# Pair attention on one core: two-chunk bursts, two-step products, and a rebuilt beginning and tail

## The chip, the core and the metric

The kernel runs on 1 core of one Trainium2 chip. The metric is device time in microseconds (us); lower is better. Everything is computed in 32-bit floats.

## The reference: what is computed

The input `r_x` is (2048, 40, 64): 2048 batches of 40 fields with 64 numbers each. For each batch all 780 pairs of fields are formed, and

```
inner  = x[:, ROW, :] * x[:, COL, :]                   # 780 products of 64 numbers
h      = relu(inner @ W1.T + b1)                       # 64 hidden units a pair
logits = h @ W2.T + b2                                 # one number a pair
attn   = softmax(logits, axis=1)                       # over the 780 pairs
pooled = sum(inner * attn, axis=1)
y      = pooled @ Wl.T + bl                            # one number a batch
```

## The kernel before, in words

Two batches lie beside each other in the 128 partitions (64 + 64 embedding numbers); such a pair is a *duo*, and there are 1024. A *step* is two duos (`STEP_DUOS`), so there are 512 steps. A *chunk* is 8 steps or 16 duos, a *round* is 32 steps or 4 chunks; there are 64 chunks and 16 rounds. The pairs are ordered by the distance between the fields: shifts 1 to 19 are full windows of 20, shift 20 is a rest of 10, and each duo's 780 pairs are two halves of 390 (`HALF`).

Per step:
- VectorE (`products`) writes the products into a ring `inner` of 8 steps: two instructions of 2 x 380 elements, and in every odd step one more of 80 for shift 20 of two steps.
- TensorE (`first_layer`, called for half 0 and half 1) multiplies them by `w1_block` in 64x32 tiles of the array. Each call is 16 matmul records of 390 columns and fills one *slot*.
- ScalarE (`relu`) empties the slot into `hidden`, 780 elements a half.
- TensorE (`score`) multiplies `hidden` of the step before by W2, again 16 records, and adds into `logit_bank`; a round's 32 steps fill its rows.

Per chunk, between two steps:
- `turn_chunk`: five 128x128 transposes bring a loaded chunk of `x_rows` into a slot; ScalarE (`copy_turned`) copies it to the ring `xt` (3 chunks), and VectorE (`extend`, `scale_rows`) repeats the first 20 fields behind the 40 and writes `x_scaled` = x times Wl.
- `gram_matrix`: 64 matmul records of 40 columns in 64x64 tiles give each batch's scaled inner products of all fields, into a slot; ScalarE (`copy_gram`) copies them to `gram_rows`, and 12 DMAs (`store_gram`) write them to memory in the order in which the softmax needs them. `load_gram` reads a round's back.

Per round: `softmax_of_round` and `sums_of_round` on VectorE, `exp_of_round` on ScalarE; maxima and sums go to `stats`. After the last round eight transposes turn `stats`, and a chain of small VectorE operations on 16 partitions merges the halves and writes `y_out`.

The order of all work is written out by hand. PSUM has three slots of two banks (`SLOTS = 3`), taken in turn by everything that TensorE writes except the scores; `place` lists the order, the counters `slots_filled` and `slots_emptied` follow it, and `wait_for_slot` makes TensorE wait until the slot of three places before has been emptied. Turns and grams stand in the loop over steps:

```
TURN_AT = -13
GRAM_AT = -5
SPREAD_AT = -3
gram_after = {max(n * CHUNK_STEPS + GRAM_AT, 1 + n): n for n in range(CHUNKS)}
turn_after = {n * CHUNK_STEPS + TURN_AT: n for n in range(2, CHUNKS)}
```

so that from step 11 on a turn and a gram follow each other after every step s with s % 8 = 3; this is called a *burst* here. At the beginning SyncE issues both halves of chunk 0, eight small loads and chunk 1 in one queue; TensorE turns chunk 0, transposes W1, turns chunk 1, and only then starts step 0. The waits of VectorE on TensorE's reading of `inner` let it run at most 8 steps ahead.

Of the kernel before, what the change touches and what calls it, by code (L numbers as in the profile page):

```python
# [6 lines left out]
ALU = mybir.AluOpType  # L7
# [3 lines left out]
P = 128  # L11
# [8 lines left out]
def pair_attention_kernel(nc, x, w1, b1, w2, b2, wl, bl, y):  # L20
# [30 lines left out]
    INNER_RING = 8  # L51
    XT_RING = 3
    SLOTS = 3

# [9 lines left out]
    with ExitStack() as ctx:  # L64
# [20 lines left out]
        x_scaled = sb("x_scaled", [P, CHUNK_DUOS * FIELDS])  # L85
# [13 lines left out]
        maxima = sb("maxima", [ROUNDS, STEP_DUOS, 2, P // 2])  # L99
        top = sb("top", [ROUNDS, STEP_DUOS, P // 2])  # L100
        down = sb("down", [ROUNDS, STEP_DUOS, 2, P // 2])
        scale = sb("scale", [ROUNDS, STEP_DUOS * P])
        part = sb("part", [ROUNDS, 3, STEP_DUOS * P])
        total = sb("total", [ROUNDS, 3, P])
        weighted_sum = sb("weighted_sum", [ROUNDS, P])
        inverse = sb("inverse", [ROUNDS, P])
        ratio = sb("ratio", [ROUNDS, P])
        y_out = sb("y_out", [ROUNDS, P])
# [8 lines left out]
        ident_ready = sem("ident_ready")  # L117
        w1_loaded = sem("w1_loaded")
# [29 lines left out]
        def inner_to(s):  # L148

            return 5 * (s // 2 + 1)  # L150


        TURN_AT = -13
        GRAM_AT = -5
        SPREAD_AT = -3

        gram_after = {max(n * CHUNK_STEPS + GRAM_AT, 1 + n): n for n in range(CHUNKS)}
        turn_after = {n * CHUNK_STEPS + TURN_AT: n for n in range(2, CHUNKS)}
        spread_after = {max(n * CHUNK_STEPS + SPREAD_AT, 1 + n): n for n in range(1, CHUNKS)}


        place = {("turn", 0): 0, ("weights", 0): 1, ("turn", 1): 2}
        for s in range(STEPS):
            place["layer", s, 0] = len(place)
            place["layer", s, 1] = len(place)
            if s in turn_after:
                place["turn", turn_after[s]] = len(place)
            if s in gram_after:
                place["gram", gram_after[s]] = len(place)
# [10 lines left out]
        EXP_AT = [4, 5]  # L180
        SUMS_AT = [13, 14]
# [3 lines left out]
        y_dram = y.rearrange("(a r k) o -> r a (k o)", a=2, k=ROUND_DUOS)  # L185
# [4 lines left out]
        def _(sp):  # L190
# [29 lines left out]
            load_chunk(0)  # L220
# [14 lines left out]
            for n in range(CHUNKS):  # L235
                if n + 2 < CHUNKS:
                    sp.wait_ge(slots_filled, count_to("turn", n))
                    load_chunk(n + 2)
                store_gram(n)
                if n % CHUNKS_PER_ROUND == CHUNKS_PER_ROUND - 1:  # L240
                    load_gram(n // CHUNKS_PER_ROUND)
# [13 lines left out]
        def _(pe):  # L255
# [12 lines left out]
            def gram_matrix(n):  # L268
                pe.wait_ge(scaled_ready, n + 1)
                wait_for_slot("gram", n)  # L270
                for m in range(GRAM_PAIRS):
                    for j in range(2):
                        duo = 2 * m + j
                        for ab in range(2):
# [4 lines left out]
                                x_scaled[rows, duo * FIELDS:(duo + 1) * FIELDS],  # L279
# [61 lines left out]
            for n in range(4 * STEP_DUOS):  # L341
                last = nc.tensor.transpose(slot[0][0:ROUNDS, n * P:(n + 1) * P], stats[:, n, :], ident[:, :])  # L342
            last.then_inc(stats_turned, 1)

        @block.scalar
        def _(act):
# [27 lines left out]
            def exp_of_round(r, j):  # L374
                if j == 0:
                    act.wait_ge(bias_ready, r + 1)
# [180 lines left out]
```

## Time and profile before

| what | value |
|---|---|
| median of 3 runs | 1144.26 us (1144.24 to 1145.02) |
| the profiled execution's own time | 1142.66 us |
| its span | 1140.8 us |
| TensorE busy | 1117.5 us, 98% |
| VectorE busy | 1053.8 us, 92% |
| ScalarE busy | 981.2 us, 86% |

The span is from the first to the last event of the program on the core; the run's own time is 1.86 us longer. PE is TensorE's matmul, PEld its weight load, DVE is VectorE, ACT is ScalarE, POOL is GpSimd, SPq is the queue of SyncE, which issues DMAs. L296 is line 296 of the kernel: L264 is the transpose of `turn_chunk`, L277 the matmul of `gram_matrix`, L296 that of `first_layer`, L316 that of `score`, L325 the transpose of W1, L342 that of `stats`; L431 and L438 are the products, L369 is the relu, L353 and L361 are the copies of a turned chunk and of a gram.

### The profile page before, as it was taken

Reading aid. Unit: us, or ns where it says so; the run is one execution under the profiler, and the core shown is the slowest. Engines: PE = TensorE matmul, PEld = TensorE weight load, DVE = VectorE, ACT = ScalarE, POOL = GpSimd, SP = SyncE. Lnnn points to the kernel's source line nnn. Section 1 sums busy time; section 2 is a strip of 40 time slices with the busy share of each in tenths; the row PEclk is TensorE's granted clock in tenths of the full one; section 3 lists DMA queues with packets and bytes.
Section 4 is the critical chain, followed back from the end, with each engine's and each line's share of the span. In section 5 each row is a group of like instructions: output and inputs, shape, how many; then the busy total and the mean of one; then the engine's idle time right before and its main releaser. Section 6 shows DMA issues by size and latency. Waiting matters only on the chain.

```text
span 1140.8 us, 63299 instructions
## 1 busy us (share of the span) xinstructions
PE 1117.5 (98%) x29001; PEld 550.5 (48%) x29001; DVE 1053.8 (92%) x1691; ACT 981.2 (86%) x1219; POOL 0.7 (0%) x6
## 2 busy tenths in 40 slices
PE   6999999999999999999999999999999999999995
PEld 3445444444444444454544544554444444544442
DVE  7999999998999989999899998999999899998983
ACT  5888888888988888888888888888889888898884
POOL 0000000000000000000000000000000000000000
PEclk9999999999999999999999999999999999999998
DMA  2231211312212221122212113122131221222110
GB/s 58 39 70 26 67 30 35 67 29 63 41 29 63 41 56 35 29 65 39 58 35 68 29 34 70 28 64 41 25 67 36 58 39 29 63 41 57 23 25 23
DMA packets 220376, 51.31 MB, mean 45 GB/s; under 512 B 216016, under 2 KB 216016, under 8 KB 220112
## 3 DMA queue, kind: packets, MB, share of 16 engines
q1 hardware_dynamic: 220112, 47.27, 20.2%
q8 instruction: 229, 3.75, 1.4%
q14 instruction: 35, 0.29, 0.1%
HBM read 34.11 MB, written 13.12 MB: 41 GB/s over the span
## 4 chain that ended last, share of the span: by engine, by line
PE 98%; DVE 1%; SPq 1%; DMA 0%; ACT 0%; issue 0%; ACTq 0%
PE slot L296 60%; PE logit_bank L316 30%; PE slot L277 4%; PE slot L264 4%; DMA x_rows<-in_r_x 0%; PE slot L342 0%; SPq L193 0%; ACT hidden L369 0%; DVE weighted L468 0%; SPq L223 0%; SPq L227 0%; SPq L225 0%; SPq L230 0%; DVE logits L448 0%; DVE row_max L452 0%
## 5 line engine op out<-in xcount | busy, mean ns | idle before, releaser
L369 ACT ACTIVATE hidden<-slot,b_col 128x780 f32<-128x780 f32 x1024 | 874.7, 909 | 118.5 <-PE slot L296 118.5
L431 DVE TENSOR_TENSOR inner<-xt 128x760 f32<-128x760 f32 x1024 | 907.8, 943 | 51.3 <-PE slot L296 50.8
L296 PE MATMUL slot<-inner,w_block 64*32 64x390 f32 x16384 | 781.4, 489 | 0.0
L296 PEld LDWEIGHTS slot<-inner,w_block 64*32 64x32 f32 x16384 | 314.1, 107 | 331.0 <-issue 271.3
L316 PE MATMUL logit_bank<-hidden,w_window 64*32 64x390 f32 x8192 | 442.9, 487 | 0.6 <-ACT hidden L369 0.6
L316 PEld LDWEIGHTS logit_bank<-hidden,w_window 64*32 64x32 f32 x8192 | 155.3, 105 | 183.5 <-ACT hidden L369 85.6
L353 ACT COPY xt<-slot 128x640 f32<-128x640 f32 x64 | 44.3, 692 | 20.4 <-PE slot L264 20.4
L264 PE MATMUL slot<-ident,x_rows 128*128 128x128 f32 x320 | 50.1, 288 | 9.7 <-DMA x_rows<-in_r_x 9.7
L438 DVE TENSOR_TENSOR inner<-xt 128x80 f32<-128x80 f32 x256 | 59.4, 232 | 0.0
L264 PEld LDWEIGHTS slot<-ident,x_rows 128*128 128x128 f32 x320 | 34.6, 143 | 49.5 <-issue 44.1
L277 PE MATMUL slot<-xt,x_scaled 64*40 64x40 f32 x4096 | 52.9, 205 | 0.0
L277 PEld LDWEIGHTS slot<-xt,x_scaled 64*40 64x40 f32 x4096 | 45.4, 117 | 11.7 <-issue 11.7
L361 ACT COPY gram_rows<-slot 128x640 f32<-128x640 f32 x64 | 44.4, 693 | 5.9 <-PE slot L277 0.4
L418 DVE TENSOR_SCALAR x_scaled<-xt,wl_col 128x640 f32<-128x640 f32 x64 | 34.8, 544 | 0.0
L448 DVE COPY logits<-logit_bank 128x780 f32<-128x780 f32 x16 | 15.5, 970 | 20.5 <-PE logit_bank L316 20.5
L468 DVE CUSTOM_DVE_ANT_1 weighted<-weight,gram 128x380 f32<-128x380 f32 x32 | 28.0, 874 | 0.8 <-ACT weight L377 0.8
L409 DVE COPY xt<-xt 128x320 f32<-128x320 f32 x64 | 20.3, 317 | 5.8 <-ACT xt L353 5.8
L377 ACT ACTIVATE weight<-logits,exp_bias 128x390 f32<-128x390 f32 x32 | 19.9, 622 | 3.6 <-DVE exp_bias L460 3.6
L452 DVE TENSOR_REDUCE row_max<-logits 128x2 f32<-128x780 f32 x16 | 15.5, 966 | 0.5
L476 DVE CUSTOM_DVE_ANT_0 weighted<-weight,gram 64x10 f32<-64x10 f32 x64 | 10.8, 169 | 1.0
L342 PE MATMUL slot<-ident,stats 128*16 128x128 f32 x8 | 1.9, 416 | 6.0 <-DVE stats L483 6.0
L377 ACT ACTIVATION_READ_ACCUMULATOR weight<-logits,exp_bias 128x1 f32 x32 | 6.4, 201 | 0.0
(28 smaller groups left out, 27.0 us busy)
## 6 DMA issues: line engine op xcount, KB each, us to landing
x_rows<-in_r_x SPq DMA_DIRECT2D x128, 160.0 KB, 3.1
gram<-gram_dram SPq DMA_DIRECT2D x32, 400.0 KB, 3.8
gram_dram<-gram_rows SPq DMA_DIRECT2D x512, 12.5 KB
gram_dram<-gram_rows SPq DMA_DIRECT2D x256, 25.0 KB
w_rows<-in_L_rec_W SPq DMA_DIRECT2D x2, 16.0 KB, 2.3
wl_col<-in_L_rec_Wl SPq DMA_DIRECT2D x2, 0.2 KB, 2.3
b_col<-in_L_rec_b SPq DMA_DIRECT2D x2, 0.2 KB, 2.3
w_window<-in_L_rec_W SPq DMA_DIRECT2D x2, 0.2 KB, 2.3
```

The lines of the kernel that those rows point to most:

```text
L264: last = nc.tensor.transpose(banks_of("turn", n)[:, t * P:(t + 1) * P], x_rows[n % 2][:, t, :, :].rearrange("p h e -> p (h e)"), ident[:, :])
L277: last = nc.tensor.matmul(banks_of("gram", n)[j * TILE:j * TILE + FIELDS, at:at + FIELDS], x_scaled[rows, duo * FIELDS:(duo + 1) * FIELDS] ...
L296: last = nc.tensor.matmul(banks[to:to + QUAD, ab * BANK:ab * BANK + HALF], w1_block[rows, of:of + QUAD], inner[rows, at:at + HALF], start= ...
L316: last = nc.tensor.matmul(logit_bank[g * QUAD:(g + 1) * QUAD, j * BANK:j * BANK + HALF], w2_window[rows, first:first + QUAD], hidden[s % R ...
L353: nc.scalar.copy(window_view(xt[n % XT_RING], 0, [[EXT, CHUNK_DUOS], [TT, U], [1, TT]]), window_view(banks_of("turn", n), 0, [[U, CHUNK_DU ...
L361: nc.scalar.copy(gram_rows[n % 2][:, :, :, :].rearrange("p a m n -> p a (m n)"), banks_of("gram", n)[:, :].rearrange("p (a n) -> p a n", a ...
L369: nc.scalar.activation(hidden[s % RING][:, half * PAIRS:(half + 1) * PAIRS].rearrange("p (a n) -> p a n", a=2), banks_of("layer", s, half) ...
L377: nc.scalar.activation(weight[:, j * HALF:(j + 1) * HALF], logits[:, j * HALF:(j + 1) * HALF], ACT.Exp, bias=exp_bias[:, j:j + 1], accum_o ...
L418: nc.vector.tensor_scalar(x_scaled[:, :].rearrange("p (d f) -> p d f", f=FIELDS), whole[:, :, 0:FIELDS], wl_col[:, 0:1], None, ALU.mult).t ...
L431: nc.vector.tensor_tensor(window_view(inner, to + half * HALF, [[PAIRS, STEP_DUOS], [SPAN, SHIFTS], [1, SPAN]]), window_view(fields, at + ...
L438: nc.vector.tensor_tensor(window_view(inner, to + SHIFTS * SPAN, [[PAIRS, duos], [HALF, 2], [1, LAST]]), window_view(fields, at, [[EXT, du ...
L468: nc.vector.tensor_tensor_reduce(out=weighted[:, 0:main].rearrange("p (d i) -> p d i", i=SPAN), in0=weight[:, of:of + main].rearrange("p ( ...
```

## The change

Five parts; the core of the diff stands below.
1. **Bursts of two chunks.** Chunks are taken in groups of 2. After steps 4, 20, 36, ... stand two turns and then two grams, where before one turn and one gram stood after every eighth step. `xt` gets 4 chunks instead of 3, `x_scaled` gets 2 buffers. SyncE stores the grams of both chunks one after the other (24 DMAs), then loads the next two chunks.
2. **Products of two steps.** In even steps VectorE makes the products of two steps, with two instructions of 4 x 380 elements and one of 80 between them. The ring `inner` has 16 steps. TensorE waits on `inner_ready` in both halves of each step.
3. **Beginning.** The second half of chunk 0 is loaded by ScalarE's queue. 14 transposes of the identity into `logit_bank` stand before the turn of chunk 0, and 14 more before step 0. Chunk 1 is turned after step 1. Chunk 0 is copied in two parts (4 duos, then 12), `extend_first` treats the first, and the products of steps 0 and 1 are made singly, with shift 20 of both behind the first instruction.
4. **Softmax of rounds.** The exponentials stand 3 and 7 steps into the next round instead of 4 and 5, the sums 15 and 21 instead of 13 and 14. In the last round there is no copy of the logits: each of the two columns of duos has its own maximum and bias, read from `logit_bank`, and ScalarE reads `logit_bank` too.
5. **Tail.** One matmul (64x64 tile, 128 columns) moves the upper 64 partitions of `stats` to the lower ones, and the merging runs on 64 partitions with 32 to 96 elements in each. `y` is stored by two DMAs whose pieces are 2 numbers (8 bytes), 512 pieces each, where one DMA had 32 pieces of 256 bytes.

```diff
-    INNER_RING = 8
-    XT_RING = 3
+    INNER_RING = 16
+    XT_RING = 4
+    GROUP = 2
     SLOTS = 3
+    FIRST_DUOS = 4
+    WARM_UP = [14, 14]
...
+        GROUP_STEPS = GROUP * CHUNK_STEPS
+        TURN_AT = -12
+        GRAM_AT = TURN_AT + GROUP_STEPS
+        SPREAD_AT = [-1, 3]
...
+        gram_after = {g * GROUP_STEPS + GRAM_AT: g for g in range(CHUNKS // GROUP)}
+        turn_after = {g * GROUP_STEPS + TURN_AT: chunks_of(g) for g in range(1, CHUNKS // GROUP)}
+        turn_after[1] = range(1, GROUP)
+        spread_after = {n // GROUP * GROUP_STEPS + SPREAD_AT[n % GROUP]: n for n in range(1, CHUNKS)}
...
-        EXP_AT = [4, 5]
-        SUMS_AT = [13, 14]
+        EXP_AT = [3, 7]
+        SUMS_AT = [15, 21]
...
-            load_chunk(0)
+            sp.dma_start(x_rows[0][:, :, 0, :], x_chunks[0, 0]).then_inc(x_loaded[0], 16)
...
+            for group in range(CHUNKS // GROUP):
+                for n in chunks_of(group):
+                    if n + 2 < CHUNKS:
+                        sp.wait_ge(slots_filled, count_to("turn", n))
+                        load_chunk(n + 2)
+                for n in chunks_of(group):
+                    store_gram(n)
+                    if n % CHUNKS_PER_ROUND == CHUNKS_PER_ROUND - 1:
+                        load_gram(n // CHUNKS_PER_ROUND)
...
             def first_layer(s, half):
-                if half == 0:
-                    pe.wait_ge(inner_ready, inner_to(s))
+                pe.wait_ge(inner_ready, inner_to(s, half))
...
+            def warm_up(count):
+                for _ in range(count):
+                    nc.tensor.transpose(logit_bank[:, 0:P], ident[:, :], ident[:, :])
             pe.wait_ge(ident_ready, 2)
+            warm_up(WARM_UP[0])
             turn_chunk(0)
             pe.wait_ge(w1_loaded, 2 * 16)
             nc.tensor.transpose(banks_of("weights", 0)[:, 0:P], w1_rows[:, :], ident[:, :]).then_inc(slots_filled, 1)
-            turn_chunk(1)
+            warm_up(WARM_UP[1])
...
                 if s in turn_after:
-                    turn_chunk(turn_after[s])
+                    for n in turn_after[s]:
+                        turn_chunk(n)
                 if s in gram_after:
-                    gram_matrix(gram_after[s])
+                    for n in chunks_of(gram_after[s]):
+                        gram_matrix(n)
...
-            for n in range(4 * STEP_DUOS):
-                last = nc.tensor.transpose(slot[0][0:ROUNDS, n * P:(n + 1) * P], stats[:, n, :], ident[:, :])
-            last.then_inc(stats_turned, 1)
+            upper = slice(TILE, P)
+            nc.tensor.matmul(slot[0][0:TILE, 0:4 * STEP_DUOS * ROUNDS], ident[upper, upper],
+                             stats[upper, :, :].rearrange("p n r -> p (n r)"), start=True, stop=True,
+                             tile_position=(TILE, 0)).then_inc(stats_turned, 1)
...
+            act.dma_start(x_rows[0][:, :, 1, :], x_chunks[1, 0]).then_inc(x_loaded[0], 16)
...
+            def shifts_to_19(to, at, duos, fields, half):
+                nc.vector.tensor_tensor(
+                    window_view(inner, to + half * HALF, [[PAIRS, duos], [SPAN, SHIFTS], [1, SPAN]]),
+                    window_view(fields, at + half * SPAN, [[EXT, duos], [0, SHIFTS], [1, SPAN]]),
+                    window_view(fields, at + half * SPAN + 1, [[EXT, duos], [1, SHIFTS], [1, SPAN]]),
+                    ALU.mult).then_inc(inner_ready, 1)
+            def first_products():
+                dve.wait_ge(xt_ready, 1)
+                for s in range(2):
+                    for half in range(2):
+                        shifts_to_19(s * STEP, s * STEP_DUOS * EXT, STEP_DUOS, xt[0], half)
+                        if s == 0 and half == 0:
+                            shift_20(0, 0, 2 * STEP_DUOS, xt[0])
             def products(s):
                 n, in_chunk = s // CHUNK_STEPS, s % CHUNK_STEPS
-                if in_chunk == 0:
-                    dve.wait_ge(xt_ready, n + 1)
+                if in_chunk == 0 or s == 2:
+                    dve.wait_ge(xt_ready, n + 2)
                 if s >= INNER_RING:
-                    dve.wait_ge(slots_filled, count_to("layer", s - INNER_RING, 1))
+                    dve.wait_ge(slots_filled, count_to("layer", s + 1 - INNER_RING, 1))
+                fields, duos = xt[n % XT_RING], 2 * STEP_DUOS
...
                 for half in range(2):
+                    shifts_to_19(to, at, duos, fields, half)
+                    if half == 0:
+                        shift_20(to, at, duos, fields)
...
+            def softmax_of_last_round(r):
+                dve.wait_ge(steps_scored, STEPS)
+                dve.wait_ge(exp_done, 2 * r)
+                for j in range(STEP_DUOS):
+                    nc.vector.reduce_max(row_max[:, j:j + 1], logit_bank[:, j * BANK:j * BANK + HALF], AX_X).then_inc(
+                        max_ready, 1)
...
-            chain(nc.vector.tensor_copy(maxima[:, :, :, :], maximum))
-            chain(nc.vector.tensor_tensor(top[:, :, :], maxima[:, :, 0, :], maxima[:, :, 1, :], ALU.max))
+            chain(nc.vector.tensor_tensor(top[:, :, :], maximum[0], maximum[1], ALU.max))
+            for half in range(2):
+                nc.vector.tensor_tensor(down[:, half, :, :], maximum[half], top[:, :, :], ALU.subtract).then_inc(
+                    down_ready, 1)
...
-            sp.dma_start(y_dram, y_out[:, :].rearrange("r (a k) -> r a k", a=2)).then_inc(y_stored, 16)
-            sp.wait_ge(y_stored, 16)
+            for a in range(2):
+                sp.dma_start(y_dram[a], y_out[a * QUAD:(a + 1) * QUAD, :, :]).then_inc(y_stored, 16)
+            sp.wait_ge(y_stored, 2 * 16)
```

## Rows read from the trace of the kernel before

**Rows 1.** The page, part 4: shares of the span on the chain that ended last.
```profile
PE 98%; DVE 1%; SPq 1%; DMA 0%; ACT 0%; issue 0%; ACTq 0%
```

**Rows 2.** Waits over the whole span: us in total, times, longest us.
```profile
DVE inner L431 <- PE slot L296: 50.8, 75, 1.6
```

**Rows 3.** Groups by form: busy us, mean ns of one, then idle before them.
```profile
L277 PE MATMUL slot<-xt,x_scaled 64*40 64x40 f32 x4096 | 52.9, 205 | 0.0
L264 PE MATMUL slot<-ident,x_rows 128*128 128x128 f32 x320 | 50.1, 288 | 9.7 <-DMA x_rows<-in_r_x 9.7
```

**Rows 4.** Timeline around one burst: start us, us, then engine, line and operation.
```profile
523.23 0.86 PE L316 MATMUL logit_bank<-hidden,w_window 64*32 64x390 f32 x16
...
523.88 1.52 PE L296 MATMUL slot<-inner,w_block 64*32 64x390 f32 x32
...
524.91 1.71 ACT L369 ACTIVATE hidden<-slot,b_col 128x780 f32<-128x780 f32 x2 [0.25 <-PE slot L296]
525.20 0.87 PE L316 MATMUL logit_bank<-hidden,w_window 64*32 64x390 f32 x16
...
525.99 0.77 PE L264 MATMUL slot<-ident,x_rows 128*128 128x128 f32 x5
...
526.69 0.83 PE L277 MATMUL slot<-xt,x_scaled 64*40 64x40 f32 x64
526.79 0.69 ACT L353 COPY xt<-slot 128x640 f32<-128x640 f32 x1 [0.17 <-PE slot L264]
...
527.45 1.54 PE L296 MATMUL slot<-inner,w_block 64*32 64x390 f32 x32
```

**Rows 5.** Timeline of the first 26 us.
```profile
0.74 1.35 SPq L193 DMA_DIRECT2D x_rows<-in_r_x  x2
...
1.17 0.29 POOL L251 TENSOR_SCALAR_AFFINE_SELECT ident<-ident 128x128 f32<-128x128 f32 x1 [0.23 <-POOL ident L249]
...
4.76 1.30 PE L264 MATMUL slot<-ident,x_rows 128*128 128x128 f32 x5 [4.76 <-DMA x_rows<-in_r_x]
...
5.86 0.42 PE L325 MATMUL slot<-ident,w_rows 128*128 128x128 f32 x1
...
6.10 0.69 ACT L353 COPY xt<-slot 128x640 f32<-128x640 f32 x1 [4.08 <-PE slot L264]
...
7.18 3.53 DVE L431 TENSOR_TENSOR inner<-xt 128x760 f32<-128x760 f32 x4
...
12.51 3.68 PE L296 MATMUL slot<-inner,w_block 64*32 64x390 f32 x64
...
25.12 1.52 PE L296 MATMUL slot<-inner,w_block 64*32 64x390 f32 x32
```

**Rows 6.** Timeline of the queue of SyncE near the end: the last gram's stores, the last load.
```profile
1101.50 5.70 SPq L204 DMA_DIRECT2D gram_dram<-gram_rows  x12
1110.40 0.82 SPq L216 DMA_DIRECT2D gram<-gram_dram  x2
```

**Rows 7.** Timeline of the tail, from the last score on.
```profile
1126.10 0.97 DVE L448 COPY logits<-logit_bank 128x780 f32<-128x780 f32 x1 [15.94 <-PE logit_bank L316]
...
1128.63 0.62 ACT L377 ACTIVATE weight<-logits,exp_bias 128x390 f32<-128x390 f32 x1 [3.58 <-DVE exp_bias L460]
...
1129.38 0.84 DVE L468 CUSTOM_DVE_ANT_1 weighted<-weight,gram 128x380 f32<-128x380 f32 x1 [0.78 <-ACT weight L377]
...
1131.97 1.88 PE L342 MATMUL slot<-ident,stats 128*16 128x128 f32 x8 [5.97 <-DVE stats L483]
1133.88 0.41 DVE L520 COPY maxima<-slot 16x256 f32<-16x256 f32 x1 [1.97 <-PE slot L342]
1134.33 0.28 DVE L521 TENSOR_TENSOR top<-maxima 16x128 f32<-16x128 f32 x1
...
1137.41 0.94 DVE L533 RECIPROCAL inverse<-total 16x128 f32<-16x128 f32 x1
...
1139.01 0.34 SPq L244 DMA_DIRECT2D out_y<-y_out  x1
```

More of the change, by code:

```diff
@@ L84, in pair_attention_kernel @@
         inner = sb("inner", [P, INNER_RING * STEP])
-        x_scaled = sb("x_scaled", [P, CHUNK_DUOS * FIELDS])
+        x_scaled = [sb(f"x_scaled{s}", [P, CHUNK_DUOS * FIELDS]) for s in range(GROUP)]
         gram_rows = [sb(f"gram_rows{s}", [P, 2, GRAM_PAIRS, FIELDS]) for s in range(2)]
@@ L146, in pair_attention_kernel, with inner_to, chunks_of @@
                                    kind="Internal").ap()
[L148 to L162, printed above, removed]
+        def inner_to(s, half):
+            return 2 + half + (2 * s if s < 2 else 3 * (s // 2) + 2)
+        GROUP_STEPS = GROUP * CHUNK_STEPS
+        TURN_AT = -12
+        GRAM_AT = TURN_AT + GROUP_STEPS
+        SPREAD_AT = [-1, 3]
+        def chunks_of(group):
+            return range(group * GROUP, (group + 1) * GROUP)
+        gram_after = {g * GROUP_STEPS + GRAM_AT: g for g in range(CHUNKS // GROUP)}
+        turn_after = {g * GROUP_STEPS + TURN_AT: chunks_of(g) for g in range(1, CHUNKS // GROUP)}
+        turn_after[1] = range(1, GROUP)
+        spread_after = {n // GROUP * GROUP_STEPS + SPREAD_AT[n % GROUP]: n for n in range(1, CHUNKS)}
+        place = {("turn", 0): 0, ("weights", 0): 1}
         for s in range(STEPS):
@@ L166, in pair_attention_kernel @@
             if s in turn_after:
-                place["turn", turn_after[s]] = len(place)
+                for n in turn_after[s]:
+                    place["turn", n] = len(place)
             if s in gram_after:
-                place["gram", gram_after[s]] = len(place)
+                for n in chunks_of(gram_after[s]):
+                    place["gram", n] = len(place)
         def count_to(*what):
@@ L509, in _ @@
             dve.wait_ge(stats_turned, 1)
-            rounds = slice(0, ROUNDS)
-            maximum = slot[0][rounds, 0:2 * P].rearrange("r (j h s) -> r j h s", j=STEP_DUOS, h=2)
-            sums = slot[0][rounds, 2 * P:8 * P].rearrange("r (n q) -> r n q", n=3)
-            chained = [ROUNDS]
+            lower = slice(0, TILE)
+            pairs = STEP_DUOS * ROUNDS
+            moved = slot[0][lower, 0:4 * pairs]
+            maximum = [stats[lower, 0:STEP_DUOS, :], moved[:, 0:pairs].rearrange("p (j r) -> p j r", j=STEP_DUOS)]
+            sums = [stats[lower, STEP_DUOS:4 * STEP_DUOS, :].rearrange("p (n j) r -> p n (j r)", n=3),
+                    moved[:, pairs:4 * pairs].rearrange("p (n q) -> p n q", n=3)]
+            chained = [ROUNDS - 1 + STEP_DUOS]
             def chain(instruction):
@@ L518, in chain @@
                 dve.wait_ge(dve_chain, chained[0])
[L520 to L531 removed]
+            chain(nc.vector.tensor_tensor(top[:, :, :], maximum[0], maximum[1], ALU.max))
+            for half in range(2):
+                nc.vector.tensor_tensor(down[:, half, :, :], maximum[half], top[:, :, :], ALU.subtract).then_inc(
+                    down_ready, 1)
+            dve.wait_ge(scale_ready, 1)
+            for half in range(2):
+                last = nc.vector.tensor_tensor(part[:, half, :, :], sums[half],
+                                               window_view(scale, half * pairs, [[0, 3], [1, pairs]], lower), ALU.mult)
+                if half == 0:
+                    last.then_inc(dve_chain, 1)
+                    chained[0] += 1
+            chain(last)
+            chain(nc.vector.tensor_tensor(total[:, :, :], part[:, 0, :, :], part[:, 1, :, :], ALU.add))
             chain(nc.vector.tensor_tensor(weighted_sum[:, :], total[:, 1, :], total[:, 2, :], ALU.add))
```

129 lines of the change are left out of this document (66 added, 63 removed).

## The prediction, made before the change was run

> **What bounds the kernel now.** I read the page first, its chain that ended last: 98% of it is TensorE's matmul [rows 1]. Then the waits: VectorE, the next busiest engine, waits 50.8 us for TensorE to give back parts of the ring `inner` [rows 2], so it runs ahead and TensorE sets the pace. ScalarE too waits before each pair of relus [rows 4]. What counts is therefore the time from one TensorE instruction group to the next, and I took that from the timeline around one burst [rows 4]: a score takes 0.65 us (523.23 to 523.88), the two halves of a layer 1.32 us (to 525.20), a step 1.97 us. A burst takes 2.25 us from the score before it to the next layer (525.20 to 527.45), less the score's own 0.65: 1.60 us. That splits into 0.14 before the turn (525.99 less 525.20 less 0.65), 0.70 from turn to gram and 0.76 from gram to layer. Then the two ends: TensorE starts step 0 at 12.51 us [rows 5], and from 1126.10 us, when the last score has ended, there is a serial chain of 14.7 us to the end of the span at 1140.8 [rows 7]. The sum below is made against the span of 1140.8 and the execution's own 1142.66 us; the median is 1144.26, 1.60 above the latter, and I subtract the same saving from it.
>
> **Part 1, bursts of two chunks.** What do two turns in a row cost? The five transposes last 0.77 us together and one lasts 0.288 on average [rows 3, 4], so they start every (0.77 - 0.288)/4 = 0.12 us. Two turns are 0.70 + 5 x 0.12 = 1.30 us, against 2 x 0.70 apart. The gram's 64 records start every (0.83 - 0.205)/63 = 0.0099 us [rows 3, 4]: two grams are 0.76 + 64 x 0.0099 = 1.39 us against 1.52. The 0.14 ahead of the turn is paid once instead of twice. A double burst is 0.14 + 1.30 + 1.39 = 2.83 us against 3.20: 0.37 saved. From the start of step 5 on, before has 61 full bursts (turns of chunks 3 to 63) and one of a gram alone (0.14 + 0.76 = 0.90): 98.5 us. After has 30 double ones and one with two grams alone (1.53): 86.4 us. Saving **12.1 us**, of which one turn has only moved to the beginning, where I count it. The lower bound: the 0.10 and 0.13 within a pair aren't a change of tile shape but something that each turn and gram pays (its wait, its new slot). Then only the 0.14 goes, after has 30 x 3.06 + 1.66 = 93.5, and the saving is 5.0. I take the upper value, since 0.12 and 0.0099 are what the trace shows inside a turn and a gram, and I see nothing else that changes at a seam except the tile shape.
>
> Does the burst now stall? Four places in a row need four slots and there are three. From the layer's start [rows 4]: relus end at about +1.9 and +2.74 (524.91 + 1.71 less 523.88), turn a starts +2.11, turn b +2.71 (needs the first relu), gram a +3.41 (needs the second), gram b +4.04. Gram b needs the copy of turn a: a copy starts 0.80 after its turn (526.79 less 525.99) and lasts 0.69, so it ends at +3.60. That is 0.44 us spare, the thinnest place. The next layer at +4.80 needs the copy of turn b, which ends at +4.3. Nothing stalls, and ScalarE is caught up when the next relu is due. The exponential now comes one step ahead of a burst (3 into a round, burst after 4); it puts ScalarE back by 0.75 us (1128.63 to 1129.38 [rows 7]) less the 0.25 idle that each step has [rows 4]: 0.5, gone again by the copies, since turn a's copy then ends at about +3.9. Priced at nothing; if it isn't hidden it costs up to 0.3 in 15 rounds, 4 us at most.
>
> SyncE: 12 stores take 5.70 us, the wait for their landing lasts until 1110.40, 3.2 us after the last issue, and the load is 0.82 [rows 6]. With 24 stores (11.7 us) the queue holds up the loads of the next two chunks, but these have a burst period of 16 x 1.97 + 2.83 = 34.3 us; loads behind stores end after some 22. The last round: stores begin about 2 us later and last 6 us longer, so the gram load is issued at about 1118.5 in the time of before and lands some 4 us later. Its reader comes at about 1128: hidden with 5 us to spare.
>
> **Part 2, products of two steps.** Four instructions of 760 elements take 3.53 us. An elementwise operation costs 1.05 ns an element (0.41 less 0.28 us for 128 elements more, a copy and a maximum of two tensors) and 0.15 fixed [rows 7], part of it overlapped, so one of 1520 saves at most 0.1 of two of 760. That frees VectorE by up to 512 x 0.1 = 50 us and gives TensorE nothing: it isn't on the chain. Priced at nothing. The cover is VectorE's lead of several steps; without it each step pair would wait for 3.5 us of products against 3.93 us of TensorE, so even then it keeps up. The second wait of `first_layer` finds its count reached and is nothing too. The softmax sits at the same step, where VectorE waits for the score of the round anyway, with a lead of 7 to 8 steps.
>
> **Part 3, beginning.** Chunk 0's halves were issued one behind the other, 1.35 us for both, and TensorE started at 4.76 [rows 5]. Two queues bring the second 0.7 earlier at best, to 4.1. But the warm-up starts when the identity is there (1.46 us) and its 14 transposes start every (1.30 - 0.42)/4 = 0.22 us: 3.1 us, so the turn starts at 4.6. Its slot was ready 1.34 later in before (6.10) and 0.80 later in the middle of the kernel; I take 1.1, so 5.7. The part copy (about 0.30) and the part extension (about 0.25) put the first product at 6.3 instead of 7.18. Products go at 0.86 each, shift 20 at 0.2: step 0 ready at 7.4 and 8.25 (its two halves), step 1 at 9.1 and 9.95; extension 0.3; then steps 2 and 3 together, half 0 by 12.1, half 1 by 13.75; scaling, extension and scaling 1.3; steps 4 and 5, half 0 by 16.9, half 1 by 18.6. TensorE is bound by VectorE here. It starts (2,1) at 13.8, ends score 1 at 15.1, step 3 with score 2 at 17.05, has to wait until 18.6 for (4,1), ends score 3 at 19.9 and the double burst at 22.75. Before, step 5 starts at 25.12 [rows 5]. Saving **2.3 us**, range 1.5 (x no earlier, all cold) to 3.0. From step 5 on TensorE has work: VectorE needs 3.5 us for two steps and TensorE 3.93.
>
> The clock: the transposes of chunk 0 and the first layers run at half rate in before. The 64 records from 12.51 last 3.68 us [rows 5], where two layers of a step in the middle last 1.32 each; the granted clock is recorded as full, the durations are those of 1.2 GHz. If the warm-up has no effect, its second half ends at 5.9 + 0.3 + 14 x 0.22 = 9.3, steps 0 and 1 lose another 0.85, and step 2 starts at about 14.2 instead of 12.1; but VectorE gives (4,1) at 18.6 in any case, and the double burst ends at 22.9 to 23.7. So the clock is worth 0.2 to 1.0 us here. The Trainium skill (TensorE: Matmul & The Clock Gate, Part 4) says that transposes do not count as busy for the clock gate. This case's before neither proves nor refutes it: the layers from 12.51 us were still slow, and what opened the clock during them can't be read off. By the rule the sum would be 17.4 less 0.2 to 1.0.
>
> **Part 5 and the last round.** VectorE after the last score: before 3.28 us to the first sum (1126.10 to 1129.38) [rows 7]: copy 0.97, maximum 0.97, two small ones 0.52, exponential 0.75. After: twice a maximum of 390 (0.56 by the rate above), two small ones and gaps, 1.12 each: 2.25. The first exponential starts at 1.12 and is there at 1.9. Saves 1.0. Moving `stats`: 1.91 before (1131.97 to 1133.88); one matmul of 128 columns is two records, 0.42 + 0.22 cold [rows 5]: 0.7, saves 1.2. Merging: before 5.13 us (1133.88 to 1139.01). After: six operations of 32 elements at 0.18, three of 96 at 0.25, the reciprocal (0.94 at 128) at about 0.35, the exponential 0.3, gaps 0.3: 2.9, saves 2.2; if fixed costs are higher (0.28 each) 1.2. Storing y: before 1.8 us from issue to the span's end. Two issues add 0.4; the landing of 512 pieces of 8 bytes isn't in the trace. Below: nothing more. Above: like the last gram store, 3.2 us instead of 1.45, plus 1.75. I take +1.1 in all, between 0.4 and 2.2, nearer to the many small pieces of the gram. The Trainium skill (DMA: Bandwidth & Descriptors, Specifications) says that writes below 512 B become read-modify-writes; both forms of the store lie below that, so it doesn't tell them apart. Tail: 1.0 + 1.2 + 2.2 - 1.1 = **3.3 us**, range 1.5 to 4.6.
>
> **The sum.** 12.1 + 2.3 + 3.3 = 17.7, less 0.3 for what the exponentials ahead of bursts may cost: 17.4. Span 1123.4, own time 1125.3, median 1144.26 - 17.4 = **1126.9 us**.
>
> **Rivals.**
> - *Seams cost what they did* (only the 0.14 goes): 7.1 less, 1134.0. For it: each turn has its own wait on a DMA and on a slot. Against: nothing of these was late in the trace. Chance 0.13.
> - *The warm-up doesn't open the clock*, the rule above: the first layers last 1.3 us a half, 1127.1 to 1127.9. Chance 0.2.
> - *The two-chunk burst stalls on the three slots.* Place: gram b waits for ScalarE's copy of turn a. With 0.44 us spare it costs nothing; if the copies come x later than that, 31 bursts cost 31x, and from x = 0.56 the gain is gone, from 0.63 it is slower by over 0.2%. A full copy behind each relu pair too late (2 x 0.69) gives 1126.9 + 43 = 1170. Chance 0.03.
> - *Part of it is given back at the ends*: no earlier x, y landing over 2 us, merging dear: 1130.5. Chance 0.1.
> - *No net change*: seams as before and both ends gain nothing, under 3 us of gain. Chance 0.03; nothing in the profile speaks for it.
> - The forecast: 0.51.
>
> Range 1123.5 to 1133: it leaves out the first, third and fifth, 0.19. A difference under 0.2% (2.3 us) is what a measurement can't tell from none. Faster 0.94, within 0.03, slower 0.03.
>
> **What would show it.** In a middle double burst: ten transposes and then 128 gram records; from the score to the next layer 0.65 + 2.83 us. 3.06 instead of 2.83 is the first rival; idle time before L277 with ScalarE's copy as releaser is the third. Start of step 5's layer at 22.75. Layer groups of 0.65 us a half in steps 0 and 1 mean an open clock. From the last score to the first issue of y's store 8.5 us (12.9 before), then 2.9 to the end. VectorE's busy time falls by some 30 to 50 us and its waits grow by as much. I would be wrong if VectorE's lead is lost after the beginning, so that TensorE waits on `inner` in the middle.

## The result: 1.3% slower, and the profile after

| | before | after |
|---|---|---|
| median | 1144.25 us (4 runs, 1143.76 to 1145.02) | 1159.26 us (4 runs, 1157.5 to 1159.69) |
| span of the profiled execution | 1140.8 us | 1157.9 us |

The ratio is 1.0129, 95% interval 1.0114 to 1.0144. I had predicted 1126.9 us (1123.5 to 1133) and gave slower a chance of 0.03.

The page of the changed kernel, parts 1, 3 and 4, beside [rows 1]:
```profile
PE 1124.2 (97%) x29023; PEld 638.7 (55%) x29023; DVE 1008.3 (87%) x1185; ACT 980.0 (85%) x1220; POOL 0.7 (0%) x6
...
q8 instruction: 231, 3.78, 1.4%
...
PE 93%; DVE 4%; issue 2%; ACT 0%; POOLq 0%; POOL 0%; ACTq 0%
```
TensorE still carries the chain, but 2% of the span is now "issue": time in which it waited for nothing that the profile shows. (The line gives VectorE 4%, but in the middle of the kernel no idle time of TensorE's matmuls has VectorE as releaser.) VectorE's busy time fell by 45 us, as foreseen, and buys nothing.

The waits of the changed kernel (us in total, times, longest us):
```profile
DVE logits L503 <- PE logit_bank L331: 108.9, 15, 9.4
...
PE slot L311 <- issue: 10.0, 12, 1.7
...
PE slot L293 <- issue: 6.0, 4, 2.1
...
PE slot L311 <- DVE inner L470: 1.2, 2, 0.7
```
VectorE waits for TensorE longer than before [rows 2]; TensorE waits for VectorE 1.2 us in all, in the beginning. Between the beginning and the last steps no idle time of its matmuls names an engine.

**Where the 17.1 us of span come from.** I split the span at two places: the start of step 5, and the end of the last score as VectorE sees it. A *period* is the 16 steps from the start of one burst's turns to the next; periods are numbered by their burst, and the one that starts at 20.03 us is number 2. Timelines of the changed kernel, the beginning and one double burst in the middle:
```profile
1.51 3.25 PE L340 MATMUL logit_bank<-ident 128*128 128x128 f32 x14 [1.51 <-POOL ident L267]
4.56 1.27 PE L280 MATMUL slot<-ident,x_rows 128*128 128x128 f32 x5
5.62 0.42 PE L346 MATMUL slot<-ident,w_rows 128*128 128x128 f32 x1
5.84 2.07 PE L340 MATMUL logit_bank<-ident 128*128 128x128 f32 x14
...
12.34 0.89 PE L311 MATMUL slot<-inner,w_block 64*32 64x390 f32 x16
13.94 0.89 PE L311 MATMUL slot<-inner,w_block 64*32 64x390 f32 x16 [0.72 <-DVE inner L470]
...
18.56 0.89 PE L311 MATMUL slot<-inner,w_block 64*32 64x390 f32 x16 [0.45 <-DVE inner L470]
19.23 0.87 PE L331 MATMUL logit_bank<-hidden,w_window 64*32 64x390 f32 x16
20.03 1.31 PE L280 MATMUL slot<-ident,x_rows 128*128 128x128 f32 x10
...
22.68 1.54 PE L311 MATMUL slot<-inner,w_block 64*32 64x390 f32 x32
```
```profile
53.52 0.86 PE L331 MATMUL logit_bank<-hidden,w_window 64*32 64x390 f32 x16
...
54.31 1.31 PE L280 MATMUL slot<-ident,x_rows 128*128 128x128 f32 x10
...
55.55 1.61 PE L293 MATMUL slot<-xt,x_scaled 64*40 64x40 f32 x128
...
57.10 1.54 PE L311 MATMUL slot<-inner,w_block 64*32 64x390 f32 x32
```
- Beginning: step 5 starts at 22.68 us instead of 25.12 [rows 5]: 2.4 us gained.
- The double burst at 20 us takes 22.68 less 19.23 less the score's 0.65 = 2.80 us against 2 x 1.60 [rows 4]; the one at 54 us is a little disturbed and takes 57.10 less 53.52 less 0.65 = 2.93. The 16 steps from burst to burst take 34.28 us where nothing goes wrong (34.43 with a softmax), against 2 x 17.35 = 34.70 before (17.50 for the half with a softmax). Gained, as in the plan: some 0.4 us a period.
- But only 9 of the 30 periods take up to 34.5 us. The 30 periods from 20.03 us on take 1060.6 us together; at 34.28, with 0.15 for each of 15 softmaxes, they would take 1030.7. That is 30 us lost, and the stretch behind them (38.09 us to the next burst) loses 3.7 more: **34 us in all**. The 19 idle times described below add up to 25 of them, and two stretches at half clock (3.4 us each) cost some 3.4; the remaining 5 to 6 us are small delays that I can't assign one by one. From step 5 to the last score the kernel takes 1121.5 us instead of 1101.0, 20.5 more, where I had predicted 12.1 less.
- Tail: 13.8 us from 1144.14 to the end, against 14.7.

This is what a lost microsecond looks like, in the timeline of the changed kernel, TensorE alone:
```profile
265.81 0.60 PE L280 MATMUL slot<-ident,x_rows 128*128 128x128 f32 x4
266.34 1.48 PE L293 MATMUL slot<-xt,x_scaled 64*40 64x40 f32 x128
269.48 1.55 PE L311 MATMUL slot<-inner,w_block 64*32 64x390 f32 x32 [1.66 <-issue]
```
and here twice as long, with the windows view of that place (us, then busy us of PE, PEld, DVE, ACT, POOL, the granted clock, DMA share, GB/s):
```profile
442.50 1.34 PE L293 MATMUL slot<-xt,x_scaled 64*40 64x40 f32 x115
445.94 0.35 PE L293 MATMUL slot<-xt,x_scaled 64*40 64x40 f32 x13 [2.10 <-issue]
446.22 2.25 PE L311 MATMUL slot<-inner,w_block 64*32 64x390 f32 x32
```
```profile
443.60:447.00 3.40, 1.30 (x63) 0.82 (x59) 3.40 (x4) 1.18 (x2) 0.00 (x0) 0.99 0.19 27
447.00:450.00 3.00, 3.00 (x48) 1.21 (x40) 3.00 (x5) 1.85 (x3) 0.00 (x0) 0.50 0.33 49
```
The second idle time falls in the middle of a gram, between records of one loop that has no wait in it. No slot, no copy, no VectorE can be late there. Behind it the granted clock was 0.50 (1.2 GHz) for some 3 us, which makes this the most expensive period (38.33 us).

**The theory.** The page has a queue q8 of kind "instruction": 231 packets of 16384 bytes. TensorE has 59218 records (matmuls, weight loads, semaphore instructions), 256.4 for each packet; before, 58662 and 229, 256.2. So q8 brings TensorE's instructions in blocks of 256. A double burst is 20 + 256 of them, the grams' 256 within 1.4 us. I looked up, for each time over 0.5 us between the starts of two records in a row, which record of the stream (modulo 256) came after it, and how long before that the last q8 packet had ended. Worked out from the trace of the changed kernel:
```
at us   idle us  record mod 256   us since the end of a q8 packet
 92.86   1.34        193            1.41
267.75   1.73        193            1.25
408.43   1.47        193            1.41
443.64   2.30        193            1.47
729.99   1.70        193            1.39
765.10   1.80        193            1.26
```
From step 5 to the last steps there are 19 such idle times outside the stretches of half clock, all at record 193, resumed 1.25 to 1.59 us after a packet. Before the change there is none over 0.5 us from step 5 to the last steps. The shortest time in which 256 records in a row start is 3.08 us before and 1.27 after.

The order of the packets says how far ahead TensorE's instructions are. Counted from 0, packet n of the changed kernel begins at the earliest 0.2 us before record 256n + 193 starts, in the middle 0.7 us after it, at most 4.4. In each of the 19 cases the packet that ended last is the one that had begun after the record 193 before, and its own length was 0.9 to 1.3 us. So the trace shows one block held ahead: from one record 193 to the next TensorE needs the packet's late start, its length and another 1.25 to 1.59 us, and the quickest such stretch took 2.87 us. All 18 stretches in which TensorE used up its 256 records in under 2.9 us ended in an idle time (0.43 to 2.3 us).

The theory, **instruction supply**: a block that is used up in less than about 3 us leaves TensorE waiting for the next. Rivals: the 24 gram DMAs behind a burst delay these packets (*store contention*); four places in a row on three slots (*slots*); the long VectorE instructions, the ring of 16 or the second wait of a step (*products*).

### The profile page after: what moved, and what is told of

It reads as the page before. It is cut to its first block, busy times and chain, and to the rows that moved or that the text cites. A ratio compares the mean times of both kernels' runs of the same rounds, so it can differ in the third digit from the quotient of the medians.

```text
span 1157.9 us, 63334 instructions
## 1 busy us (share of the span) xinstructions
PE 1124.2 (97%) x29023; PEld 638.7 (55%) x29023; DVE 1008.3 (87%) x1185; ACT 980.0 (85%) x1220; POOL 0.7 (0%) x6
## 4 chain that ended last, share of the span: by engine, by line
PE 93%; DVE 4%; issue 2%; ACT 0%; POOLq 0%; POOL 0%; ACTq 0%
PE slot L311 57%; PE logit_bank L331 28%; PE slot L293 4%; PE slot L280 3%; DVE inner L470 3%; DVE weighted L536 0%; PE logit_bank L340 0%; DVE inner L463 0%; DVE x_scaled L459 0%; ACT hidden L396 0%; DVE row_max L522 0%; DVE weighted L544 0%; DVE xt L450 0%; PE slot L366 0%; DVE round_stats L525 0%
## 5 line engine op out<-in xcount | busy, mean ns | idle before, releaser
L311 PE MATMUL slot<-inner,w_block 64*32 64x390 f32 x16384 | 870.3, 489 | 11.1 <-issue 10.0
L470 DVE TENSOR_TENSOR inner<-xt 128x1520 f32<-128x1520 f32 (+1 forms) x514 | 874.6, 1728 | 0.6
L311 PEld LDWEIGHTS slot<-inner,w_block 64*32 64x32 f32 x16384 | 387.4, 107 | 326.8 <-issue 220.3
L331 PE MATMUL logit_bank<-hidden,w_window 64*32 64x390 f32 x8192 | 531.1, 488 | 1.9 <-issue 1.3
L331 PEld LDWEIGHTS logit_bank<-hidden,w_window 64*32 64x32 f32 x8192 | 191.3, 105 | 143.9 <-issue 52.8
L293 PE MATMUL slot<-xt,x_scaled 64*40 64x40 f32 x4096 | 48.9, 205 | 6.0 <-issue 6.0
L379 ACT COPY xt<-slot 128x640 f32<-128x640 f32 (+1 forms) x65 | 41.4, 689 | 6.7 <-PE slot L280 6.7
L280 PE MATMUL slot<-ident,x_rows 128*128 128x128 f32 x320 | 42.7, 280 | 0.0
L450 DVE COPY xt<-xt 128x320 f32<-128x320 f32 (+1 forms) x64 | 20.3, 317 | 0.0
L409 ACT ACTIVATE weight<-logits,exp_bias 128x390 f32<-128x390 f32 x30 | 18.6, 620 | 0.0
L340 PE MATMUL logit_bank<-ident 128*128 128x128 f32 x28 | 5.3, 367 | 1.5 <-POOL ident L267 1.5
```

The source lines that it names most:

```text
L280: last = nc.tensor.transpose(banks_of("turn", n)[:, t * P:(t + 1) * P], x_rows[n % 2][:, t, :, :].rearrange("p h e -> p (h e)"), ident[:, :])
L293: last = nc.tensor.matmul(banks_of("gram", n)[j * TILE:j * TILE + FIELDS, at:at + FIELDS], x_scaled[n % GROUP][rows, duo * FIELDS:(duo + 1 ...
L311: last = nc.tensor.matmul(banks[to:to + QUAD, ab * BANK:ab * BANK + HALF], w1_block[rows, of:of + QUAD], inner[rows, at:at + HALF], start= ...
L331: last = nc.tensor.matmul(logit_bank[g * QUAD:(g + 1) * QUAD, j * BANK:j * BANK + HALF], w2_window[rows, first:first + QUAD], hidden[s % R ...
L379: copied = nc.scalar.copy(window_view(xt[n % XT_RING], first * EXT, [[EXT, last - first], [TT, U], [1, TT]]), window_view(banks_of("turn", ...
L450: nc.vector.tensor_copy(whole[:, duos, FIELDS:EXT], whole[:, duos, 0:SPAN]).then_inc(xt_ready, 1)
```

## The experiments

All times are medians beside runs of the kernel before on the same chip (1143.8 or 1144.2); ratios are to that kernel.

**e1: the second gram four steps later.**
```diff
-        gram_after = {g * GROUP_STEPS + GRAM_AT: g for g in range(CHUNKS // GROUP)}
+        for g in range(CHUNKS // GROUP):
+            gram_after[g * GROUP_STEPS + GRAM_AT] = [g * GROUP]
+            gram_after[g * GROUP_STEPS + GRAM_AT + 4] = [g * GROUP + 1]
```


> The changed kernel, but the second gram of each pair stands 4 steps later (after steps 8, 24, 40, ... instead of 4, 20, 36, ...), so that no burst has more than 20 + 128 TensorE instructions. Instruction supply (TensorE runs out of instructions in and just behind a burst of 276 in 2.8 us): the 32 us of stalls vanish, and what is left is the beginning (2.4 us), the tail (0.9) and the seams that still go (31 pairs by about 0.1): 1144.3 - 6.5 = about 1138 us. Store contention (the DMAs of the grams delay TensorE's instructions): the same DMAs still follow, in two parts; some stalls stay, 1143 to 1155. Long vector instructions or the ring of 16 steps: nothing changes there, 1158 to 1160.

Measured: 1136.3 us, ratio 0.9933 (0.9918 to 0.9948). 26 of 30 periods are 34.55 or 34.70 us within 0.1. Moving 128 of 276 instructions is enough; three idle times over 0.5 us are left, each at record 193. There the 256 records had taken 4.2 to 4.8 us, but the packet had begun 2.5 to 2.7 us late.

**e2: the stores later.**
```diff
             def store_gram(n):
+                if n < CHUNKS - GROUP:
+                    sp.wait_ge(slots_emptied, count_to("layer", n // GROUP * GROUP_STEPS + GRAM_AT + 3, 1))
```


> The changed kernel, but SyncE starts the 24 stores of a pair of grams only when the relus of the third step behind the burst are done, some 8 us later; the last pair is stored as before. Instruction supply: the stalls lie 4 to 6 us behind the start of a burst whatever the stores do, 1158 to 1160 us. Store contention: the stalls vanish or move behind the stores; if they vanish 1159.3 - 32 = 1127, if they move no less than half stay, and they then lie 10 us or more behind the start of a burst.

Measured: 1155.3 us (1153.0 to 1159.6), ratio 1.0113 (1.0092 to 1.0134). The timelines of TensorE and of SyncE's queue around one burst (it began at 89.8 us):
```profile
92.77 0.52 PE L313 MATMUL slot<-inner,w_block 64*32 64x390 f32 x6
94.14 1.17 PE L313 MATMUL slot<-inner,w_block 64*32 64x390 f32 x18 [0.84 <-issue]
```
```profile
100.75 3.56 SPq L219 DMA_DIRECT2D gram_dram<-gram_rows  x9
```
TensorE starts again 4.4 us into the burst, 6.6 us before the first store. Store contention isn't the cause. The runs scatter by 6.6 us and the median lies 4 below the changed kernel's; the profiled execution has 18 idle times at 193, no period over 36.4 us and no half clock. Whether the stores add something to single stalls stays open.

**e3: bursts of one chunk, the rest as changed.**
```diff
+        gram_after = {max(n * CHUNK_STEPS - 5, 3 + 2 * n): [n] for n in range(CHUNKS)}
+        turn_after = {n * CHUNK_STEPS - 13: [n] for n in range(2, CHUNKS)}
+        turn_after[1] = [1]
```
SyncE stores each chunk's gram by itself again, as in the kernel before.

> The changed kernel with one-chunk bursts where the kernel before has them (a turn and a gram after every eighth step); all the rest as changed: double products, ring of 16, beginning, tail. Instruction supply: no stalls in the middle; beginning 2.4 and tail 0.9 us better than before: about 1141 us. Long vector instructions or the doubled waits of the first layer as cause: the stalls stay, 1150 to 1162.

Measured: 1139.1 us, ratio 0.9959 (0.9944 to 0.9974); no idle time over 0.5 us. Everything but the double bursts together is a gain of 4.7 us.

**e4: products of single steps.**
```diff
                 for half in range(2):
-                    shifts_to_19(to, at, duos, fields, half)
-                    if half == 0:
-                        shift_20(to, at, duos, fields)
+                    shifts_to_19(to, at, STEP_DUOS, fields, half)
+                if s % 2:
+                    shift_20(to - STEP, at - STEP_DUOS * EXT, 2 * STEP_DUOS, fields)
```


> The changed kernel, but from step 2 on VectorE makes the products of single steps and TensorE waits on them once a step, as before; bursts, ring size, beginning and tail as changed. Instruction supply and store contention: 1158 to 1161 us, stalls as in the changed kernel. Long vector instructions or the second wait of a step as cause: about 1127 to 1130 us. VectorE's waits for TensorE shrink by some 35 us in any case.

Measured: 1157.5 us, ratio 1.0124 (1.0105 to 1.0143), 18 idle times, all at 193. The kernel differs from its description in one thing: the wait instruction in the second half stayed, with a count that is already reached. e11 is free of it.

**e5: half of each gram, same places.**
```diff
-                for m in range(GRAM_PAIRS):
+                for m in range(0, GRAM_PAIRS, 2):
```


> The changed kernel with its double bursts, but every second pair of duos is left out of the grams (64 TensorE records of a pair of grams instead of 128, so 148 instructions in a burst instead of 276); half of the gram values are therefore old contents of the slots. The burst still takes four places of three slots and the same copies and stores. Instruction supply: the work left out is 32 x 0.63 = 20 us and the 32 us of stalls vanish too, 1159.3 - 52 = about 1107 us, every period of 16 steps 33.65 us. Slots (TensorE waits for ScalarE because four places in a row need three slots): the stalls stay, about 1139 us.

Measured: 1112.3 us (two runs). No idle time over 0.5 us; 28 of 30 periods are 33.87 or 34.0 us. The work left out is 0.41 us a period, not 0.63, 13 us in all; 1159.3 less 13 less the 34 lost gives 1112. With the stalls kept it would be 1146. The burst still has four places in a row on three slots, so slots are out.

**e6: the same kernel, 128 instructions later.**
```diff
-    WARM_UP = [14, 14]
+    WARM_UP = [14, 78]
```


> The changed kernel with 64 more transposes of the identity ahead of step 0, so that everything behind them stands 128 instructions later in TensorE's stream; nothing else. Instruction supply in blocks of 256 instructions (16384 bytes): in the changed kernel the periods of 16 steps whose burst begins at instruction 50 to 200 of a block are 34.9 to 38.3 us and those at 203 to 31 are 34.3 to 34.8. Shifted by 128, the periods that were long become short and the other way round (those that began at 203 to 31 now begin at 75 to 159 and are 35.3 or more); the time is 1159 + 7 for the transposes = about 1166. A cause that lies in the work (slots, DMA, VectorE, the round) leaves the long periods where they are.

Measured: 1163.5 us (two runs), 17 idle times over 0.5 us, all at record 193 again. Nothing of the work behind step 0 differs, yet the long periods are others. Worked out from both traces, the period's number with the record (modulo 256) at which its burst begins and its length in us:
```
period      changed kernel      e6
   2         31   34.28      159   36.12
   6          0   34.28      128   35.96
  10        226   34.28       98   35.03
   8        113   35.51      241   34.29
  17        110   37.24      238   34.43
  26        106   35.62      234   34.30
```
This is the test I trust most: a cause in the work would have stayed in its period.

**e12: the kernel before, grams twice.**
```diff
-                for m in range(GRAM_PAIRS):
+                for m in [m for m in range(GRAM_PAIRS) for again in range(2)]:
```


> The kernel before the change, with each matmul of the grams issued twice in a row (same result): a burst of one turn and one gram then has 10 + 256 instructions in 2.2 us. The work itself costs 64 x 0.63 = 40 us: 1184. Instruction supply: on top of it the periods of 8 steps (17.35, so 17.98 with the double gram) stall wherever the burst begins in the wrong part of a block, half of 63 by about 1 us or more: 1205 to 1250, with idle time of TensorE that nothing on the core releases. Stalls that come from the changed kernel's order (two turns, two grams, ring sizes, stores of two chunks) are absent here: 1184.

Measured: 1230.2 us (two runs), ratio 1.0750 (1.0728 to 1.0771). 30 idle times over 0.5 us, all at record 193, together 34 us; a burst of it in TensorE's timeline:
```profile
63.76 1.44 PE L277 MATMUL slot<-xt,x_scaled 64*40 64x40 f32 x128
65.13 0.85 PE L296 MATMUL slot<-inner,w_block 64*32 64x390 f32 x6
66.84 1.20 PE L296 MATMUL slot<-inner,w_block 64*32 64x390 f32 x21 [0.85 <-issue]
```
46 us over the 1184 of the work itself (its undisturbed periods of 8 steps are 17.96 us, 0.61 longer than before), in a schedule that never stalled. Dense instructions alone are sufficient.

**e7: e1, and y stored in rows.**
```diff
+            pe.wait_ge(ratio_ready, 1)
+            for j in range(STEP_DUOS):
+                last = nc.tensor.transpose(slot[1][0:ROUNDS, j * TILE:(j + 1) * TILE],
+                                           ratio[:, j * ROUNDS:(j + 1) * ROUNDS], ident[0:TILE, 0:TILE])
...
-            for a in range(2):
-                sp.dma_start(y_dram[a], y_out[a * QUAD:(a + 1) * QUAD, :, :]).then_inc(y_stored, 16)
+            sp.dma_start(y_dram, y_out[:, :].rearrange("r (a k) -> r a k", a=2)).then_inc(y_stored, 16)
```


> The split grams of e1, and at the end two transposes of the quotients (64x16 each) into PSUM, the last addition reading them there, and y stored by one DMA of 32 pieces of 256 bytes as before the change, in place of two DMAs with 1024 pieces of 8 bytes. Pieces as cause of the long landing: the store takes 1.8 us from issue to the end of the span instead of 5.9, the transposes cost 0.6 to 0.8, so 3.3 us less than e1: about 1133.0 us. If the landing was long for another reason (the state of the core at the end), 1137.

Measured: 1132.9 us, ratio 0.9905 (0.9892 to 0.9919). Its tail, and the store of the changed kernel (span 1157.9):
```profile
1127.97 0.10 PEld L374 LDWEIGHTS slot<-ident,ratio 64*16 64x16 f32 x2 [2.83 <-DVE ratio L619]
1127.98 0.38 PE L374 MATMUL slot<-ident,ratio 64*16 64x64 f32 x2 [2.43 <-DVE ratio L619]
1128.39 0.34 DVE L621 TENSOR_SCALAR y_out<-slot,bl_col 16x128 f32<-16x128 f32 x1 [0.47 <-PE slot L374]
1128.76 0.34 SPq L263 DMA_DIRECT2D out_y<-y_out  x1
```
```profile
1152.04 0.87 SPq L260 DMA_DIRECT2D out_y<-y_out  x2
```
From the issue to the end 1.7 us (span 1130.5) against 5.9. The size and the number of the pieces (32 of 256 bytes against 1024 of 8) changed together; no run separates them. From the start of the quotient to the issue it takes 1.0 us (1127.74 to 1128.76) instead of 0.5 in the changed kernel (1151.55 to 1152.04); the difference is the price of the transposes.

**e8 and e9: both grams together where the block allows it.**
```diff
+            if g + 1 in TOGETHER:
+                gram_after[at] = [g * GROUP, g * GROUP + 1]
```
`TOGETHER` lists nine groups; the others are split as in e1, and both kernels store y as e7 does.

> As e7, but in the nine periods whose burst begins at instruction 203 to 31 of a block in the changed kernel (and at the first burst) both grams stay together; in the others the second stands 4 steps later. Instruction supply: these nine periods take 34.28 instead of 34.55 us and get no stall, 2.4 us less than e7: about 1130.6 us. If the position in the block does not decide, some of the nine stall by 1 to 2 us each, and it is slower than e7.

> e8 again with its slip mended: there the grams stayed together one period too late, in periods whose burst begins at instruction 20 to 110 of a block. Now the nine are those whose burst begins at 238 to 31 (and at 20), by the changed kernel's trace. Instruction supply: these nine periods take 34.28 (34.43 with a softmax) instead of 34.55 (34.70) and none stalls: 9 x 0.27 = 2.4 us less than e7, about 1130.4 us. If the position in the block isn't what decides, 1132 to 1136.

Measured: e8 1135.1 us, ratio 0.9929 (0.9915 to 0.9942); e9 1130.5 us, ratio 0.9877 (0.9863 to 0.9892). In e8 my list was one period off: four of its nine joined bursts, which begin at 50 to 87, took 35.1 to 35.2 us and one at 80 took 35.75. In e9 six of the nine take 34.28 to 34.43, three 34.6 to 34.7, and no idle time exceeds 0.5 us. Nine joins in better chosen periods are worth 4.6 us; e9 beats both kernels and is the fastest of the study, if only by 2.3 us over e7, whose interval touches its own.

**e10: e7 without the warm-up** (`WARM_UP = [0, 0]`).

> e7 without the 28 transposes of the identity at the beginning. My prediction's sum: the first layers then run at half rate, but VectorE holds the fourth step's second half until 18.6 us anyway, so 0.2 to 1.0 us slower than e7: 1133.0 to 1133.9 us; the layers of step 0 take 1.3 us a half. If the warm-up is what the beginning gains by: 2 us slower or more.

Measured: 1133.3 us, ratio 0.9901 (0.9884 to 0.9917): by the time no difference from e7. In its timeline:
```profile
7.39 5.15 PE L314 MATMUL slot<-inner,w_block 64*32 64x390 f32 x64 [1.63 <-DVE inner L471]
...
18.95 0.89 PE L314 MATMUL slot<-inner,w_block 64*32 64x390 f32 x16 [0.31 <-DVE inner L478]
```
The first two steps take 5.15 us at half rate, and the second half of step 4 starts 0.4 us later than with the warm-up (18.56). VectorE hides the rest. The middle isn't quite e7's: the bursts begin at other records (232 instead of 31 at the first double one), and one idle time of 1.15 us at record 193 has come in.

**e11: e7 with products of single steps and one wait.** The edit is e4's, and `first_layer` waits only in half 0 from step 2 on.

> e7 with products of single steps from step 2 on, and one wait of TensorE on them in a step. With no stalls in the way this shows what two-step products give by themselves. My prediction: nothing in the middle, since TensorE sets the pace; here the beginning loses, since steps 2 and 3 are released together after both: 0 to 2 us slower than e7, 1133 to 1135. If two-step products matter through VectorE's lead: slower by more, with idle time of TensorE on inner in the middle.

Measured: 1134.2 us, ratio 0.9911 (0.9896 to 0.9925). Step 2 starts at 14.54 instead of 12.34, the first double turn 0.9 us later; the periods are the same 34.55 and 34.70. In the middle two-step products give nothing.

## Why the prediction was wrong

- **The step that failed** is the paragraph "Does the burst now stall?". I checked slots, ScalarE's copies, SyncE's queue and VectorE's lead, each by its rows, and concluded "nothing stalls". Those four held. I didn't ask whether TensorE gets its instructions fast enough: q8 stood on the page, a gram's records every 0.0099 us were in my own sum, and I multiplied them to 256 in 1.4 us without seeing the rate. What the runs showed in its place: TensorE stops up to 2.3 us for its next block of 256 instructions. It cost 34 us (all of it is gone in e5), against a gain of 13.5 between step 5 and the last score, where I had predicted 12.1.
- The rival on the other side named the right place, the double burst, with the wrong mechanism (copies too late) and 0.03.
- Seams: 2.83 us a double burst predicted, 2.80 measured; 0.37 us a pair saved predicted, 0.42 measured in undisturbed periods. Right; the 0.3 for the exponentials ahead of bursts was nothing (a softmax costs 0.15 a period, as before); "seams cost what they did" is refuted.
- Beginning: 22.75 predicted for step 5, 22.68 measured; (2,1) at 13.94 and (4,1) at 18.56 were predicted 13.8 and 18.6. Clock: 0.2 to 1.0 predicted, 0.4 (e10).
- Tail up to the store: from the last score to the issue 12.9 before, 7.9 measured, 8.5 predicted. The mis-sized term is the landing of y: +1.1 taken, 2.2 as upper bound, +4.1 measured (5.9 less 1.8), for 1024 pieces. The gram stores that I bounded it by have pieces of 80 bytes and more, y's are 8 bytes. The tail gained 0.9 instead of 3.3.
- Two-step products and the second wait at nothing: right (e11), apart from 0.9 us in the beginning.

The Trainium skill (Runtime: NRT & Kernel Launch, Instruction fetch mechanics) says that an engine's instructions come in 16 KiB blocks of 256 over a queue of its own. The trace agrees: 16384-byte packets, 256.4 records each. It also calls the cost of crossing a block mostly hidden, which holds for the kernel before and not here: up to 2.3 us a crossing.

What stays open: why a packet begins right at record 193 in one block and 4.4 us behind it in another. Together with the packet's length and the time in which the block before was used up, that delay makes a stall 0.5 or 2.3 us long, and a long one lets a few slower blocks stall too (e1, and e10's 1.15 us). Moving the stores didn't shorten it: its median is 0.7 us in e2 as well.

## What to carry to other kernels

Count instructions as well as columns: here TensorE's stream comes 256 instructions at a time, and each time 256 of a block were used up in under 2.9 us in the changed kernel, it stalled. Gather small matmuls only as far as that allows; splitting one burst in two turned 1159.3 us into 1136.3 at the price of 0.27 us a period. Idle time with "issue" as releaser in the middle of a loop without waits is the sign. And keep the last store's pieces few and large: 1024 pieces of 8 bytes cost 4 us here, two small transposes 0.5.

## What the hardware showed that I had not expected

- TensorE stops at one fixed place of its instruction stream: 19 of 19 idle times in the changed kernel, 18 in e2, 18 in e4, 17 in e6 and 30 in e12 at record 193 of 256, resumed 1.2 to 1.6 us after the end of a 16384-byte packet.
- So an edit that only shifts the stream moves the stalls (e6), and two schedules that join nine pairs of grams each can differ by 4.6 us (e8, e9).
- Transposes opened TensorE's clock: the first 14 start every 0.21 us (3.25 us), the second 14, after nothing but transposes, take 2.07 us, and their starts come every 0.109 us (2.4 GHz) from 6.6 us on. The Trainium skill (TensorE: Matmul & The Clock Gate, Part 4) says they don't count as busy; this trace contradicts it.
- An idle time of 2.1 us in a gram was followed by a granted clock of 0.50 (1.2 GHz) for 3 us; that period lost 4 us. The same idle time at the same place in e4 (2.1 us, ending at 450.1) was not: the clock stayed at 1.00 there. So the half clock is no sure price of such a stall.
